# Second layer of a four-layer cross-attention kernel: transposes issued one projection behind the next scores, the output projection in the second and fourth quarter

## The chip, the cores and the metric

The kernel runs on one core of a Trainium2 chip. A core has engines with instruction streams of their own: TensorE (matmuls and transposes, writing to eight PSUM banks), VectorE, ScalarE, GpSimd, and SyncE, which here only issues DMAs. They order each other by semaphores. The metric is the device time of one execution in microseconds (us); lower is better.

## What is computed

Four layers of cross attention run one after the other on x (16 blocks of 128 x 512) with one context (16 x 128 x 512): a latent layer, a grouped-query layer (the one changed here), a cross layer with an MLP, a latent layer again. The second layer is, cut to what matters:

```python
B, L, S = (4, 256, 256)        # 32 heads, 8 key/value heads, 16 wide; per 256 rows
q = hidden_state @ Wq + bq
k = encoder_hidden_state @ Wk + bk
v = encoder_hidden_state @ Wv + bv
...
scores = jnp.einsum('bkgld,bksd->bkgls', q, k) * scale
scores = scores + encoder_attention_mask[:, :, None, :, :]
attn = jax.nn.softmax(scores, axis=-1)
out = jnp.einsum('bkgls,bksd->bkgld', attn, v)
out = out.transpose(0, 3, 1, 2, 4).reshape(b, l, H)
out = out @ Wo + bo
x = out + hidden_state
mu = jnp.mean(x, axis=-1, keepdims=True); var = jnp.var(x, axis=-1, keepdims=True)
return (x - mu) * jax.lax.rsqrt(var + EPS) * gamma + beta
```

(The kernel groups the rows its own way: 16 blocks of 128 rows, taken as 8 pairs, with a mask and context for each.)

## The kernel before

Everything is fp32; weight matmuls run in three passes of a split into a rounded high part and a low rest (`three_passes`, L325, called from everywhere, so L327 carries most matmuls of all kinds). The order of each engine is written out by hand, one function for an engine and a layer: `pe_gqa`, `act_gqa`, `dve_gqa`, `pool_gqa`, `sp_gqa`.

The second layer is a loop over 8 pairs of blocks. A pair has four rounds (k = 0 to 3), each 16 score groups of 128 x 128 on four partition strips: round k treats block k % 2 of the pair and heads half k // 2. One round is:

- scores S(k) on TensorE (`pe_scores`, L418, 24 matmuls of 256 columns) into PSUM banks 0 to 3;
- `dve_max` (L1017) on VectorE for r = 0 to 3: adds the mask, writes the negated scores to SBUF, keeps the maximum, frees the bank;
- `act_exp` (L733) on ScalarE for r = 0 to 3, four exponentials each, with sums;
- `dve_invert` (L1042): reciprocals of the sums, one half (two r) at a time; `pool_norm` (L1370) on GpSimd multiplies them in;
- transposes T(k) (`pe_turn_probs`, L460, 16 of 128 x 128) into four banks; `act_probs` copies banks 0 and 2 to SBUF, `dve_probs` banks 1 and 3;
- attention A(k) (`pe_attend`, L471); its bank is evacuated by `act_heads` (L748, high part) and then `dve_heads` (L1068, low part, which frees the bank and counts as the evacuation).

Banks 4 to 7 are a ring: `begin` (L217) gives every projection, transpose group and attention the next bank, and waits until the one four places back has been evacuated. So TensorE can be no more than four results ahead of the slower of its readers, in the order in which they are issued.

Between the rounds stand the projections: queries Q, keys KG and values VG of the next pair in this layer, keys KC and values VC of the next layer (computed ahead here and stored to DRAM), the turning of the next pair's rows X, and the output projection of a block, O (`pe_out`, L502). `pe_out` waits for the evacuated attention of both rounds of its block: rounds 0 and 2 for the even one, 1 and 3 for the odd one. VectorE adds residual and bias to it (`dve_out`, L1169) and takes its moments; GpSimd normalises twice (`pool_root`, `pool_again`) and adds the next bias (`pool_bias`); SyncE stores and loads (`sp_gqa`, L1677). The context of the next pair is loaded into the place of the present one's (`sp_c`, L1558), once the last projection that reads it has been filled.

TensorE's order in a middle pair before is: S1 T0 X O(odd) A0 KG KC | S2 T1 Q KC A1 | S3 T2 VG VC A2 | S0 of the next pair, T3 O(even) Q A3 VC. Here a bar ends a quarter, and each T stands right behind the next round's scores.

## Time and profile before

| | us |
|---|---|
| median of 3 runs | 2543.95 (2542.75 to 2545.22) |
| the profiled execution | 2550.35 |
| its span, first to last instruction | 2548.4 |
| TensorE busy in the span | 2451.6 (96%) |
| VectorE, ScalarE, GpSimd busy | 1237.0, 1086.8, 1126.2 |
| second layer's loop, first S1 to the last pair's end | 378.8 (809.37 to 1188.17) |

A matmul's end is modelled, so a busy share of TensorE says little of how well it is used; starts are better read against each other. A row of a timeline gives start, length, engine, line, operation, operands, count, and in brackets how long the engine was idle before it and what released it. In a table of stretches the column of the clock is the granted TensorE clock as a share of 2.4 GHz, the mean over the stretch.

### The profile page before, as it was taken

The numbers are of one execution on the slowest core, as the hardware profiler recorded it, in microseconds if no ns is written. First come the engines' busy times: TensorE is split into PE (matmuls) and PEld (weight loads), VectorE is DVE, ScalarE is ACT, GpSimd is POOL, SyncE is SP. The second block draws the span as 40 slices with busy tenths as digits, with TensorE's granted clock in tenths as the row PEclk, the third lists the DMA queues.
The fourth block names the chain that finished last, engine by engine and source line by source line (L and its number), as shares of the span: only waits on it lengthen the run. The fifth ranks groups of instructions, "written<-read, shape, count | busy, mean of one in ns | idle before, by whom it ended". The sixth has DMA issues, their size and how long they took to land.

```text
span 2548.4 us, 48703 instructions
## 1 busy us (share of the span) xinstructions
PE 2451.6 (96%) x18464; PEld 2053.4 (81%) x18464; DVE 1237.0 (49%) x3296; ACT 1086.8 (43%) x3712; POOL 1126.2 (44%) x1972
## 2 busy tenths in 40 slices
PE   7999999999999999998888999999999999999999
PEld 6888887888888878887777788888888888788887
DVE  5565655333224667676666432233555555432332
ACT  4555654111114877877777111111555555311111
POOL 3444445600053887778786630033345433640000
PEclk9999999999999999998899999999999999999999
DMA  4221212311033223323443320122112111330110
GB/s 151 72 67 59 98 37 89 90 50 50 18 100 118 99 84 124 110 92 111 152 161 121 116 91 1 50 88 75 35 63 80 51 51 51 104 100 1 50 33 17
DMA packets 106774, 198.07 MB, mean 78 GB/s; under 512 B 8304, under 2 KB 35632, under 8 KB 103600
## 3 DMA queue, kind: packets, MB, share of 16 engines
q1 hardware_dynamic: 106544, 194.97, 23.0%
q8 instruction: 149, 2.44, 0.4%
q14 instruction: 81, 0.66, 0.1%
HBM read 136.22 MB, written 58.72 MB: 76 GB/s over the span
## 4 chain that ended last, share of the span: by engine, by line
PE 79%; ACT 9%; DVE 4%; POOL 4%; DMA 2%; issue 1%; SPq 0%; DVEq 0%; POOLq 0%
PE banks L327 70%; PE banks L468 5%; ACT plain_high L743 5%; PE banks L498 3%; ACT plain_low L743 2%; POOL plain_high L1378 2%; ACT plain_work L808 1%; DVE stats L1158 1%; PE banks L522 1%; ACT plain_work L727 1%; DMA rounded_work<-ctx_split 1%; POOL rounded_high L318 0%; DMA plain_high<-attention_w 0%; DVE plain_work L1173 0%; DVE plain_high L1028 0%
## 5 line engine op out<-in xcount | busy, mean ns | idle before, releaser
L327 PE MATMUL banks<-rounded_work,rounded_low 128*128 128x512 f32 (+1 forms) x2688 | 533.6, 355 | 9.5 <-DVE rounded_low L1190 9.0
L327 PEld LDWEIGHTS banks<-rounded_work,rounded_low 128*128 128x128 f32 x2688 | 445.7, 199 | 73.6 <-issue 12.4
L836 ACT ACTIVATE plain_work<-banks,columns 128x512 f32<-128x512 f32 x192 | 132.4, 690 | 863.9 <-PE banks L327 856.9
L327 PE MATMUL banks<-rounded_work,rounded_high 128*128 128x512 f32 (+1 forms) x2400 | 482.4, 355 | 2.9 <-DMA rounded_work<-ctx_split 2.9
L327 PEld LDWEIGHTS banks<-rounded_work,rounded_high 128*128 128x128 f32 x2400 | 396.3, 191 | 68.0 <-issue 4.4
L1347 DVE CAST rounded_work<-plain_work 128x512 fp32r<-128x512 f32 x192 | 104.5, 544 | 687.6 <-ACT plain_work L836 672.4
L1378 POOL TENSOR_SCALAR plain_high<-plain_high,inv_sum 128x128 f32<-128x128 f32 (+1 forms) x768 | 298.3, 412 | 304.0 <-DVE inv_sum L1050 303.7
L327 PE MATMUL banks<-rounded_low,rounded_work 128*128 128x512 f32 x1728 | 416.3, 392 | 0.0
L327 PE MATMUL banks<-rounded_high,rounded_work 128*128 128x512 f32 (+1 forms) x1728 | 393.1, 379 | 2.4 <-DVE rounded_work L1349 2.4
L327 PEld LDWEIGHTS banks<-rounded_low,rounded_work 128*128 128x128 f32 x1728 | 321.5, 188 | 70.7 <-issue 4.4
L327 PEld LDWEIGHTS banks<-rounded_high,rounded_work 128*128 128x128 f32 x1728 | 310.1, 189 | 65.7 <-issue 5.7
L1378 POOL TENSOR_SCALAR plain_low<-plain_low,inv_sum 128x128 f32<-128x128 f32 (+1 forms) x512 | 221.2, 455 | 286.4 <-DVE inv_sum L1050 286.3
L1524 POOL TENSOR_TENSOR plain_work<-plain_work 128x512 f32<-128x512 f32 x48 | 68.1, 1449 | 584.0 <-DMA plain_work<-x 392.1
L743 ACT ACTIVATE plain_low<-banks,neg_max 128x128 f32<-128x128 f32 (+1 forms) x512 | 209.4, 459 | 28.0 <-DVE neg_max L1032 28.0
L743 ACT ACTIVATE plain_high<-plain_high,neg_max 128x128 f32<-128x128 f32 x512 | 198.0, 391 | 33.9 <-DVE neg_max L1028 33.9
L1032 DVE TENSOR_REDUCE neg_max<-banks 128x2 f32<-128x512 f32 (+1 forms) x320 | 204.8, 682 | 15.7 <-PE banks L457 15.7
L1349 DVE TENSOR_TENSOR rounded_work<-plain_work,rounded_work 128x512 fp32r<-128x512 f32 x192 | 165.5, 862 | 6.6
L468 PE MATMUL banks<-ident,plain_high 128*128 128x128 f32 x1024 | 139.4, 285 | 25.5 <-POOL plain_high L1378 19.6
L468 PEld LDWEIGHTS banks<-ident,plain_high 128*128 128x128 f32 x1024 | 113.3, 144 | 44.9 <-issue 23.8
L1050 DVE RECIPROCAL inv_sum<-row_sum 128x4 f32<-128x4 f32 (+1 forms) x224 | 41.6, 187 | 221.0 <-ACT plain_high L743 126.2
L327 PEld LDWEIGHTS banks<-rounded_work 32*128 32x128 f32 x3072 | 102.0, 186 | 43.6 <-issue 41.7
L327 PE MATMUL banks<-rounded_work 32*128 32x256 f32 (+1 forms) x3072 | 124.1, 291 | 10.2 <-DVE rounded_work L1104 7.5
(106 smaller groups left out, 3118.7 us busy)
## 6 DMA issues: line engine op xcount, KB each, us to landing
plain_work<-x SPq DMA_DIRECT2D x96, 256.0 KB, 3.0
plain_work<-mlp_w SPq DMA_DIRECT2D x96, 256.0 KB, 2.7
rounded_work<-ctx_split SPq DMA_DIRECT2D x16, 1024.0 KB, 5.9
u<-plain_work SPq DMA_DIRECT2D x48, 256.0 KB, 2.1
plain_work<-u SPq DMA_DIRECT2D x12, 1024.0 KB, 7.0
x<-plain_work SPq DMA_DIRECT2D x48, 256.0 KB, 2.2
plain_work<-attention_w SPq DMA_DIRECT2D x44, 256.0 KB, 2.7
ctx_split<-rounded_work SPq DMA_DIRECT2D x8, 1024.0 KB, 5.6
```

What stands on the lines that cost most here:

```text
L327: mm = pe.matmul(dst, lhs(i), rhs(j), start=first and n == 0, stop=last and n == 2, skip_group_check=True)
L468: mm = pe.transpose(dst[:, t * P:(t + 1) * P], pr[:, r, t * P:(t + 1) * P], ident[:, :])
L498: mm = pe.matmul(dst[32 * r:32 * r + 32, i * P:(i + 1) * P], v, pt[:, r, at:at + P], start=t == 0, stop=t == n_t - 1, skip_group_check=True)
L522: mm = pe.transpose(dst[:, r * P:(r + 1) * P], u_nat[:, r, f * P:(f + 1) * P], ident[:, :])
L743: last = act.activation(pr[:, r, part], pr[:, r, part] if gqa else PS[:, r, part], ACT.Exp, scale=-1.0 if gqa else 1.0, bias=neg_max[:, R ...
L836: act.activation(gelu[:, j % 2, :], bank(key), ACT.Gelu_apprx_tanh, bias=col(m.y, 28 + j)).then_inc(evac_of(key), 1)
L1032: dve.tensor_reduce(neg_max[:, R % 2, r, 0:y.segs], src.rearrange("p (g n) -> p g n", g=y.segs), AX.X, ALU.max, negate=True).then_inc(maxe ...
L1050: dve.reciprocal(inv_sum[:, R % 2, 2 * half:2 * half + 2, 0:y.segs], row_sum[:, R % 2, 2 * half:2 * half + 2, 0:y.segs]).then_inc(inverted, 1)
L1347: dve.tensor_copy(G[:, j % 4, 0, :], gelu[:, j % 2, :]).then_inc(g_hi, 1)
L1349: dve.tensor_tensor(G[:, j % 4, 1, :], gelu[:, j % 2, :], G[:, j % 4, 0, :].bitcast(F32), ALU.subtract).then_inc(g_ready, 1)
L1378: last = pool.tensor_scalar(part, part, inv_sum[:, R % 2, r, g:g + 1], 1.0, ALU.mult, ALU.mult)
L1524: last = pool.tensor_tensor(res[:, r, :], res[:, r, :], wide_bias, ALU.add)
```

## The change

- TensorE: after each S comes first a projection (VC in the first and third quarter, O in the second and fourth), then T. O moves from the first quarter to the second (odd block) and, in the fourth, ahead of T3 (even block); VC moves from the third quarter and the lap's end to the first and third; KC, KG and VG are spread anew. X is waited for by the queries, not by the keys (`pe_rows`).
- ScalarE and VectorE get a round of their own for this layer (`act_late_round`, `dve_late_round`): ScalarE does exponentials 0 and 1, then both copies of turned banks, then exponentials 2 and 3. VectorE does maxima 0 and 1, something handed in (`lower`), maximum 2, something handed in (`beside`), maximum 3, the lower reciprocals, its two copies, something handed in (`behind`), the upper reciprocals. Handed in as `lower` are the heads of round 1 (in round 3), of round 2 (in round 0 of the next pair) and of round 3 (in round 1 of the next pair); the heads of round 0 stay behind the work of round 1.
- The output's addition (`dve_add`) is split from its moments (`dve_added`). Both VC copies are on VectorE.
- GpSimd and SyncE follow: bias, root and repeat change places among the normalisations; the context load stands behind the stores of keys and values and waits for VG instead of VC.

```diff
@@ -348,8 +348,12 @@
                 pe.wait_ge(aff_split, 2 * p + 2)
             else:
                 pe.wait_ge(c_loaded, 16 * (c_index(y, p) + 1))
-                wait_evac(pe, ("X", y.n, p, 0))
-                wait_evac(pe, ("X", y.n, p, 1))
+                if y.kind == LATENT:
+                    pe_rows(pe, y, p)
+
+        def pe_rows(pe, y, p):
+            for i in range(2):
+                wait_evac(pe, ("X", y.n, p, i))
 
         def pe_turn_x(pe, y, p):
...
             if y.kind == CROSS and i == 0:
                 pe_inputs(pe, y, p)
+            if y.kind == GQA and i == 0:
+                pe_rows(pe, y, p)
...
             if p == 0:
                 pe_weights(pe, y, "kv" if y.kind == GQA else "v")
+            if y.kind == CROSS and i == 0:
+                pe.wait_ge(c_loaded, 16 * (c_index(L[1], p) + 1))
@@ -627,41 +635,40 @@
             for p in range(PAIRS):
                 more = p + 1 < PAIRS
                 pe_scores(pe, y, p, 1)
+                if more:
+                    pe_values(pe, L[2], p + 1, 0)
                 pe_turn_probs(pe, y, p, 0)
                 pe_turn_x(pe, *((y, p + 1) if more else (L[2], 0)))
+                if more:
+                    pe_keys(pe, y, p + 1, 0)
+                pe_attend(pe, y, p, 0)
+                if more:
+                    pe_keys(pe, L[2], p + 1, 0)
+                pe_scores(pe, y, p, 2)
                 if p:
                     pe_out(pe, y, 2 * p - 1)
-                pe_attend(pe, y, p, 0)
-                if more:
-                    pe_keys(pe, y, p + 1, 0)
-                    pe_keys(pe, L[2], p + 1, 0)
-                pe_scores(pe, y, p, 2)
                 pe_turn_probs(pe, y, p, 1)
                 pe_queries(pe, *((y, p + 1) if more else (L[2], 0)), 0)
-                if more:
-                    pe_keys(pe, L[2], p + 1, 1)
                 pe_attend(pe, y, p, 1)
                 pe_scores(pe, y, p, 3)
+                if more:
+                    pe_values(pe, L[2], p + 1, 1)
                 pe_turn_probs(pe, y, p, 2)
                 if more:
-                    pe_values(pe, y, p + 1, 0)
-                    pe_values(pe, L[2], p + 1, 0)
+                    pe_keys(pe, L[2], p + 1, 1)
                 else:
                     pe_queries(pe, L[2], 0, 1)
                 pe_attend(pe, y, p, 2)
                 if more:
-                    pe_scores(pe, y, p + 1, 0)
-                else:
-                    pe_scores(pe, L[2], 0, 0)
+                    pe_values(pe, y, p + 1, 0)
+                pe_scores(pe, *((y, p + 1) if more else (L[2], 0)), 0)
+                pe_out(pe, y, 2 * p)
                 pe_turn_probs(pe, y, p, 3)
-                if not more:
+                if more:
+                    pe_queries(pe, y, p + 1, 1)
+                else:
                     pe_turn_x(pe, L[2], 1)
-                pe_out(pe, y, 2 * p)
-                if more:
-                    pe_queries(pe, y, p + 1, 1)
                 pe_attend(pe, y, p, 3)
-                if more:
-                    pe_values(pe, L[2], p + 1, 1)
 
         def pe_cross(pe, y):
@@ -858,6 +865,15 @@
         def act_warm(act, n, func):
 
             act.activation(warm[:, n:n + 1], minus_half[:, :], func)
+
+        def act_late_round(act, y, p, k, turned, of):
+
+            act_exp(act, y, p, k, 0)
+            act_exp(act, y, p, k, 1)
+            act_probs(act, of, *turned, 0)
+            act_probs(act, of, *turned, 2)
+            act_exp(act, y, p, k, 2)
+            act_exp(act, y, p, k, 3)
 
         def act_latent(act, y):
@@ -936,42 +952,35 @@
...
+                act_late_round(act, y, p, 1, (p, 0), y)
+                for i in range(2):
+                    act_x(act, *((y, p + 1) if more else (L[2], 0)), i)
+                if more:
+                    act_keys(act, y, p + 1, 0)
+                act_heads(act, y, p, 0)
+                if more:
+                    act_keys(act, L[2], p + 1, 0)
+                act_late_round(act, y, p, 2, (p, 1), y)
+                act_queries(act, *((y, p + 1) if more else (L[2], 0)), 0)
+                act_heads(act, y, p, 1)
+                act_late_round(act, y, p, 3, (p, 2), y)
+                if more:
+                    act_keys(act, L[2], p + 1, 1)
+                else:
+                    act_queries(act, L[2], 0, 1)
+                act_heads(act, y, p, 2)
+                if more:
+                    act_values(act, y, p + 1, 0)
+                act_late_round(act, *((y, p + 1) if more else (L[2], 0)), 0, (p, 3), y)
+                if more:
+                    act_queries(act, y, p + 1, 1)
+                else:
...
+                        act_x(act, L[2], 1, i)
                 act_heads(act, y, p, 3)
...
@@ -1039,9 +1048,9 @@
         def dve_probs(dve, y, p, k, r):
             dve_copy(dve, ("T", y.round(p, k), r), prob_t(y)[:, r, :])
 
-        def dve_invert(dve, y, p, k):
+        def dve_invert(dve, y, p, k, halves=(0, 1)):
             R, u = y.round(p, k), y.use(p, k)
-            for half in range(2):
+            for half in halves:
                 for r in (2 * half, 2 * half + 1):
                     if y.kind == GQA:
@@ -1166,17 +1175,37 @@
                 dve.tensor_scalar(neg_mean[:, i:i + 1], moments[:, i, 0:1], -1.0, None, ALU.mult)
                 dve.tensor_copy(spread[:, i:i + 1], moments[:, i, 1:2]).then_inc(moments_ready, 1)
 
-        def dve_out(dve, y, b):
+        def dve_add(dve, y, b):
             key = ("out", y.n, b)
             wait_filled(dve, key)
             dve.wait_ge(biased, y.b0 + b + 1)
             dve.tensor_tensor(hidden[:, b % 2, :], bank(key), hidden[:, b % 2, :], ALU.add).then_inc(evac_of(key), 1)
-            wait_evac(dve, key)
+
+        def dve_added(dve, y, b):
+            wait_evac(dve, ("out", y.n, b))
             dve_moments(dve, y, b)
+
+        def dve_out(dve, y, b):
+            dve_add(dve, y, b)
+            dve_added(dve, y, b)
 
         def dve_again(dve, y, b):
             dve.wait_ge(norm_ready, b + 1)
             dve_moments(dve, y, b, 1)
+
+        def dve_late_round(dve, y, p, k, turned, lower, beside, behind, of):
+
+            dve_max(dve, y, p, k, 0)
+            dve_max(dve, y, p, k, 1)
+            lower()
+            dve_max(dve, y, p, k, 2)
+            beside()
+            dve_max(dve, y, p, k, 3)
+            dve_invert(dve, y, p, k, (0,))
+            dve_probs(dve, of, *turned, 1)
+            dve_probs(dve, of, *turned, 3)
+            behind()
+            dve_invert(dve, y, p, k, (1,))
 
         def dve_latent(dve, y):
@@ -1258,45 +1287,59 @@
...
+            for i in range(2):
+                dve_values(dve, L[2], 0, i)
...
+                def values(i):
+                    if more:
+                        dve_values(dve, L[2], p + 1, i)
+
+                def last_heads():
+                    if p:
+                        dve_heads(dve, y, p - 1, 3)
+
+                def cross_keys():
+                    if more:
+                        dve_keys(dve, L[2], p + 1, 0)
+
+                def odd_out():
+                    if p:
+                        dve_add(dve, y, 2 * p - 1)
+
+                def odd_moments():
+                    if p:
+                        dve_again(dve, y, 2 * p - 2)
+                        dve_added(dve, y, 2 * p - 1)
+
+                def even_moments():
+                    if p:
+                        dve_again(dve, y, 2 * p - 1)
+                    dve_added(dve, y, 2 * p)
+
+                dve_late_round(dve, y, p, 1, (p, 0), last_heads, lambda: values(0), nothing, y)
+                for i in range(2):
+                    dve_x(dve, *((y, p + 1) if more else (L[2], 0)), i)
+                if more:
+                    dve_keys(dve, y, p + 1, 0)
                 dve_heads(dve, y, p, 0)
...
+                dve_late_round(dve, y, p, 2, (p, 1), cross_keys, odd_out, odd_moments, y)
                 dve_queries(dve, *((y, p + 1) if more else (L[2], 0)), 0)
+                dve_late_round(dve, y, p, 3, (p, 2), lambda: dve_heads(dve, y, p, 1), lambda: values(1), nothing, y)
...
+                else:
...
+                dve_late_round(dve, *((y, p + 1) if more else (L[2], 0)), 0, (p, 3), lambda: dve_heads(dve, y, p, 2),
+                               lambda: dve_add(dve, y, 2 * p), even_moments, y)
...
+                else:
+                    for i in range(2):
+                        dve_x(dve, L[2], 1, i)
+            dve_heads(dve, y, PAIRS - 1, 3)
...
@@ -1466,12 +1509,7 @@
                 more = p + 1 < PAIRS
                 pool_norm(pool, y, p, 1)
                 if p:
-                    pool_again(pool, y, 2 * p - 2)
-                    pool_root(pool, y, 2 * p - 1)
-                pool_norm(pool, y, p, 2)
-                if p:
-                    pool_again(pool, y, 2 * p - 1)
-                pool_bias(pool, y, 2 * p)
+                    pool_bias(pool, y, 2 * p - 1)
                 if p < 4:
                     split_tile(pool, ("qo", 2), p)
                 if not more:
@@ -1479,12 +1517,19 @@
                     pool.wait_ge(v_stored, 16 * PAIRS)
                     split_tile(pool, ("qo", 2), 4)
                     split_tile(pool, ("qo", 2), 5)
+                pool_norm(pool, y, p, 2)
+                if p:
+                    pool_again(pool, y, 2 * p - 2)
+                    pool_root(pool, y, 2 * p - 1)
                 pool_norm(pool, y, p, 3)
-                pool_bias(pool, y, 2 * p + 1)
+                pool_bias(pool, y, 2 * p)
                 if not more:
                     split_tile(pool, ("qo", 2), 6)
                 pool_norm(pool, *((y, p + 1) if more else (L[2], 0)), 0)
+                if p:
+                    pool_again(pool, y, 2 * p - 1)
                 pool_root(pool, y, 2 * p)
+            pool_bias(pool, y, B - 1)
 
         def pool_cross(pool, y):
@@ -1679,24 +1724,23 @@
             for t, name in ((gamma, "gamma"), (beta, "beta")):
                 sp.dma_start(t, ins[f"L1_xattn_{name}"].rearrange("(a n) -> a n", a=1).broadcast_to([P, D])).then_inc(gb_loaded, 16)
             sp_ahead(sp, 0)
+            wait_filled(sp, ("V", 2, 0, 1))
+            sp_c(sp, y, 1)
             for p in range(PAIRS):
                 more, far = p + 1 < PAIRS, p + 2 < PAIRS
                 if more:
-                    wait_filled(sp, ("V", 2, p, 1))
-                    sp_c(sp, y, p + 1)
                     if p:
                         sp.wait_ge(s_free[3], y.use(p - 1, 3) + 1)
                     sp_qk_mask(sp, p + 1)
                 if p < 4:
                     load_tile(sp, ("qo", 2), p)
                 if not more:
-                    wait_filled(sp, ("V", 2, p, 1))
+                    wait_filled(sp, ("Q", 1, p, 1))
                     sp_cross_keys(sp, 0)
                     sp_mask(sp, L[2], 0)
                     load_tile(sp, ("qo", 2), 4)
                     load_tile(sp, ("qo", 2), 5)
                 if p:
-                    sp_values_ahead(sp, p)
                     sp_store_h(sp, y, 2 * p - 2)
                 if more:
                     wait_filled(sp, ("X", y.n, p + 1, 1))
@@ -1711,10 +1755,14 @@
                     load_tile(sp, ("qo", 2), 6)
                 if p:
                     sp_store_h(sp, y, 2 * p - 1)
+                if more:
+                    sp_ahead(sp, p + 1)
+                if far:
+                    wait_filled(sp, ("V", 1, p + 1, 0))
+                    sp_c(sp, y, p + 2)
+                if p:
                     sp_store_u(sp, y, 2 * p - 1)
                     sp_next_hidden(sp, y, 2 * p + 1)
-                if more:
-                    sp_keys_ahead(sp, p + 1)
 
```

## Rows read from the trace of the kernel before

**Rows 1.** Stretches (laps 0, 6, 7): length; busy PE, PEld, DVE, ACT, POOL; clock; DMA.

```profile
809.37:857.47 48.10, 42.96 (x465) 37.73 (x464) 30.07 (x170) 37.59 (x160) 28.09 (x71) 0.96 0.22 75
...
1095.38:1142.71 47.33, 44.70 (x478) 38.61 (x477) 33.44 (x183) 37.38 (x160) 36.56 (x83) 1.00 0.31 104
1142.71:1188.17 45.46, 36.54 (x405) 30.73 (x404) 29.59 (x144) 34.16 (x155) 37.66 (x78) 0.85 0.30 100
```

**Rows 2.** Timeline of TensorE, lap 5: start, length, operation, count, idle before and releaser.

```profile
1048.05 1.00 PE L327 MATMUL banks<-rounded_work 32*128 32x256 f32 x24
1048.99 1.97 PE L468 MATMUL banks<-ident,plain_high 128*128 128x128 f32 x16
1050.79 1.36 PE L359 MATMUL banks<-ident,plain_work 128*128 128x128 f32 x8
1052.43 3.00 PE L327 MATMUL banks<-rounded_high 128*128 128x512 f32 x12 [0.29 <-ACT plain_work L727]
1055.37 1.08 PE L498 MATMUL banks<-plain_work 128*32 128x128 f32 x32
1056.38 1.69 PE L327 MATMUL banks<-rounded_work,rounded_high 128*128 128x256 f32 x12
1057.91 3.04 PE L327 MATMUL banks<-rounded_work,rounded_low 128*128 128x256 f32 x24
1060.88 1.00 PE L327 MATMUL banks<-rounded_work 32*128 32x256 f32 x24
...
1071.46 0.66 PE L468 MATMUL banks<-ident,plain_high 128*128 128x128 f32 x4
...
1074.67 2.87 PE L327 MATMUL banks<-rounded_high,rounded_work 128*128 128x128 f32 x24
...
1082.20 1.09 PE L468 MATMUL banks<-ident,plain_high 128*128 128x128 f32 x8
...
1085.58 3.01 PE L327 MATMUL banks<-rounded_high 128*128 128x512 f32 x12
...
1095.38 1.00 PE L327 MATMUL banks<-rounded_work 32*128 32x256 f32 x24
```

**Rows 3.** Page, costliest groups: busy us and mean ns of one, idle before.

```profile
L1378 POOL TENSOR_SCALAR plain_high<-plain_high,inv_sum 128x128 f32<-128x128 f32 (+1 forms) x768 | 298.3, 412 | 304.0 <-DVE inv_sum L1050 303.7
L743 ACT ACTIVATE plain_high<-plain_high,neg_max 128x128 f32<-128x128 f32 x512 | 198.0, 391 | 33.9 <-DVE neg_max L1028 33.9
```

**Rows 4.** Timeline of ScalarE, the same lap.

```profile
1065.56 0.58 ACT L727 ACTIVATE plain_work<-banks 128x512 f32<-128x512 f32 x1
```

**Rows 5.** Timeline of VectorE, the same lap.

```profile
1049.06 0.29 DVE L1028 CUSTOM_DVE_ANT_0 plain_high<-banks,plain_work 128x128 f32<-128x128 f32 x1
...
1049.91 0.29 DVE L1028 CUSTOM_DVE_ANT_0 plain_high<-banks,plain_work 128x128 f32<-128x128 f32 x1
...
1054.35 1.29 DVE L1127 TENSOR_TENSOR rounded_work<-banks,rounded_work 128x512 fp32r<-128x512 f32 x2 [0.62 <-ACT rounded_work L812]
...
1073.61 0.60 DVE L1077 SCALAR_TENSOR_TENSOR rounded_high<-banks,columns,rounded_high 128x128 fp32r<-128x128 f32 x2
```

**Rows 6.** Timeline of TensorE, behind three lone gaps elsewhere.

```profile
789.99 1.49 PE L327 MATMUL banks<-rounded_work 32*128 32x256 f32 x24 [1.89 <-issue]
...
1438.76 4.58 PE L327 MATMUL banks<-rounded_high,rounded_work 128*128 128x512 f32 x12 [2.37 <-DVE rounded_work L1349]
...
1780.92 1.01 PE L327 MATMUL banks<-rounded_work 32*128 32x256 f32 x24 [2.04 <-DVE rounded_work L1104]
```

**Rows 7.** Stretches behind the same gaps.

```profile
790.00:795.40 5.40, 5.40 (x49) 5.17 (x50) 3.47 (x32) 3.03 (x16) 0.00 (x0) 0.68 0.00 0
...
1438.70:1442.00 3.30, 3.24 (x8) 2.59 (x9) 3.23 (x4) 0.69 (x1) 3.13 (x4) 0.52 0.14 22
...
1780.90:1784.00 3.10, 3.08 (x37) 2.64 (x38) 1.98 (x4) 1.25 (x5) 0.00 (x0) 1.00 0.00 0
```

**Rows 8.** Chain of waits, in lap 0: start, length, what.

```profile
810.69 7.42 DMA rounded_work<-ctx_split
```

54 lines of the change are left out of this document (6 added, 48 removed).

## Prediction

> **What bounds the kernel now.** I read the page's busy shares first: TensorE is by far the busiest. The change touches only the second layer, so I went there with the table of stretches, cut at the first scores of each pair (a lap: from S1 of one pair to S1 of the next). Laps 1 to 6 run from 857.47 to 1142.71, 47.54 us each; lap 0 takes 48.10, lap 7 45.46 with a granted clock of 0.85 [rows 1]. In a middle lap TensorE is busy 44.70 of 47.33, with the clock at 1.00, GpSimd 36.56, ScalarE 37.38, VectorE 33.44: no other engine fills a lap.
>
> Then TensorE's own timeline shows what the lap could lose [rows 2]. Sixteen transposes at their own pace take 1.80 us (1048.99 to 1050.79). In the third quarter they take 3.21 (1071.46 to 1074.67), in the fourth 3.38 (1082.20 to 1085.58), and the eight of the input rows 1.64 where half of 1.80 would do. That is 1.41 + 1.58 + 0.74 = 3.73 us of waiting and refilling a lap; without it the lap would be 43.6. Six laps of 3.7 are 22 us, the most that this change could bring.
>
> **The change part by part.** I name TensorE's steps S (scores), T (transposes), A (attention), Q, KG and VG (this layer), KC and VC (next layer's keys and values), X (rows), O (output). The new lap is S1 VC T0 X KG A0 KC | S2 O(odd) T1 Q A1 | S3 VC T2 KC A2 VG | S0 O(even) T3 Q A3. TensorE's work is the same; only its order and what it waits for differ.
>
> *Removed: the waits of T.* The transposes of a quarter now start S + one 12-step projection after the next scores, 0.94 + 2.94 = 3.9 us [rows 2]. In a quarter the sixteen exponentials take 16 x 0.39 = 6.2 us of ScalarE [rows 3]; now the two lower ones come first and the copies after them, all done 9.15 after the scores (worked out below), and GpSimd's last eight multiplications take 8 x 0.41 = 3.3 at most (a mean that mixes two sizes): 12.8 with 0.3 for the inverse. The last T is due 13.5 + 1.3 after its scores (quarter 9.6 + 3.9). So I take all 3.73 as gone. In the first and third quarter, 12 us long, GpSimd's root and repeat stand ahead of the multiplications, and T is due 16 us after its scores there. The bias is due when O is done; GpSimd has 10 us a lap to spare [rows 1], so I cost it at nothing; late by x, it costs x.
>
> *Added: X waits for copies, KC for X.* The ring has four banks, so KC needs the bank of the first X. VectorE frees it only after ScalarE has done exponentials 0 and 1, two copies (0.5 each [rows 4]) and exponentials 2 and 3. In time from S1: maxima from 1.0, 0.85 each; exponentials from 1.95, the first two done at 5.05, copies at 6.05, all done at 9.15; VectorE's subtraction starts 0.62 after ScalarE's copy of X and takes 0.69 for the first [rows 5], free at 10.5. KC would be due at 0.94 + 2.94 + 1.80 + 0.9 + 0.3 + 1.53 + 1.01 = 9.4 (the 0.3 is the second X waiting for VectorE's copy). So a wait of 1.0 besides the 0.3.
>
> *Added: O(even) waits for the heads, and this decides.* `pe_out` waits for the evacuated attention of both quarters of its row, the newer being A2. VectorE's half of that evacuation (`dve_heads`) is now handed to the next round as `lower`: behind the maxima of scores 0 and 1 of S0. TensorE however issues O right behind S0. Those maxima start 1.0 us after S0 and take 1.70, the heads 0.60 [rows 5]: free at 3.3, O starts at about 3.45 where S0 ended at 0.94. A wait of 2.5 us in each lap. Queued behind it on TensorE are T3, Q, A3 and the next S1; on VectorE the addition of O, and behind that maximum 3 and the inverses. What is late next is only O itself; nothing else runs on TensorE meanwhile. Before, the heads of A2 were done well ahead, since O came after T3. O(odd) has no such wait: its last heads are done in the first quarter.
>
> Two more bank waits (Q behind T, KC behind T2) are 0.1 each. New waits: 0.3 + 1.0 + 0.2 + 2.5 = 4.0, and 0.2 for refilling the array: lap 43.6 + 4.2 = 47.8, against 47.54, so +0.26. Freed waits and new ones cancel.
>
> *The clock.* A gap of 2.5 us is new for a middle lap. Three lone gaps in dense work show what follows one [rows 6, 7]: after 1.89 us idle the granted clock is 0.68 over the next 5.4 us, after 2.37 it is 0.52, near 1.2 GHz, after 2.04 it stays at 1.00, 2.4 GHz. The twelve 512-wide matmuls after the second took 4.58 against 2.94 [rows 2, 6]: 1.6 us lost, on the path, as O stands behind the gap. Two of three gaps: 1.1 per lap. Bounds 0 and 1.6. The Trainium skill (TensorE: Matmul & The Clock Gate, section "Why this matters for your kernels") warns of long idle stretches of TensorE, not of pauses as short as these; by it the clock would hold here, and two of three rows disagree. With it: +0.26 - 0 instead of +1.36 per lap. The laps go by the rows: 6 x 1.36 = 8.2.
>
> *Lap 0.* The next pair's VC now comes straight behind S1, and needs that pair's context, whose place is free only when this pair's VC has been computed. The load was issued at 810.69 and took 7.42, to 818.1 [rows 8]; before, T0, X and A0 ran meanwhile. Now TensorE stands still from 810.3 to 818.1, then VC runs at the low clock (4.45 with its overlap, to 822.55). VectorE holds maximum 3 until it has copied VC. T fills a bank in 0.6; ScalarE copies it at 823.2 and the third at 824.05, does exponentials 2 and 3 by 827.65, X is freed 1.3 later, KC runs to 832.0. The other three quarters have 43.6 - 12.1 = 31.5 of work and 2.9 of waits: S1 of lap 1 at 866.4, not 857.47, +8.9; with the clock behind O, +10.0. A context landing sooner and VC at full clock would make it 6.5 or so.
>
> *Later context loads* are issued when VG is done, at S0, and needed 13 us later; they took 7.4 with other transfers beside them [rows 8]. The keys' and values' stores now start about 1.5 us before it. I cost it at nothing; late by x, it costs x a lap.
>
> *Lap 7 and the next layer's head.* T1 no longer waits behind row work, and O(14) waits 2.4 for its heads. I take 0, between -3 and +3.
>
> *Moved at no cost:* one value copy from ScalarE to VectorE (0.6 us of 14 idle [rows 1]); root, repeat and bias on GpSimd; on SP the context load now stands behind the stores of keys and values and a store of the result.
>
> **The sum.** 10.0 + 8.2 + 0 = +18.2 us on the profiled execution, whose own time is 2550.35 (2548.4 and 1.95 around it), 6.4 over the median of 2543.95. The difference carries over: 2562.1.
>
> **The rivals.**
> - *The clock holds:* seven laps lose 1.1 less, 18.2 - 7.7 = 10.5, giving 2554.5. For it: the gap of 2.04 and the 1.00 of every middle lap; against: two of three gaps. 0.25. This is what the rule of the Trainium skill above would give.
> - *Faster: the heads are free in time.* If VectorE reached A2's heads before S0, O would not wait: lap 45.3, six laps -13.4, lap 0 +6.4, sum -7.0: 2536.9. It decides at a wait w of 7w = 7.0, 1.0 us. Against it stands the order: maxima 0 and 1 alone are 1.7 long. 0.07.
> - *No change:* laps stay at 47.5 with the clock up, and lap 0 loses 5 or less: 2546 or so. 0.11.
> - *The context load becomes the bound.* Taking twice its 7.42 beside the stores, it is late by 1.8 in each of six laps: 18.2 + 10.8, 2573. For it: 1.5 MB more at the same time; against: 13 us of room. 0.05.
>
> **How the numbers follow.** Forecast 2562.1, chance 0.52. A measurement of this kernel can't tell less than 0.2% (5.1 us) from no change. Slower: 0.52 + 0.25 + 0.05 = 0.82; same 0.11; faster 0.07. Low end: no fall of the clock, lap 0 at 7, lap 7 at -3: +5.0, 2549. High end: the clock falls in all seven laps (+3.5) and lap 7 gives +3: 2569.
>
> **What would show it.** Right: eight waits of TensorE of about 2.5 us at the output on VectorE's heads; about 1 us a lap on VectorE's subtraction of X; no wait of T on GpSimd in laps 1 to 6; laps of 48 to 49.5 with a clock between 0.93 and 1.00; lap 0 near 57 to 58 with one wait of 7 to 8 us on the context. Wrong: laps near 45 (the heads don't hold O), or waits of VC on the context in every lap.

## The result, and the profile after

The changed kernel takes 2572.97 us (median of 4 runs, 2569.33 to 2573.43); the kernel before took 2544.59 beside it. The ratio is 1.0112 with a 95% interval of 1.0097 to 1.0126: slower by 28.4 us, where +18.2 was forecast. The sign and the main mechanism came out as predicted, the size did not: 2572.97 lies above the range, which ended at 2569.

The profiled execution took 2572.71 with a span of 2570.5. TensorE's busy share is still 96%, so it shows nothing. The laps do, each cut from the S1 of one pair to the S1 of the next as in [rows 1]. Columns: stretch, length, busy time of PE (TensorE), PEld (its weight loads), DVE (VectorE), ACT (ScalarE) and POOL (GpSimd), granted clock, DMA share, GB/s moved. The stretches are laps 0, 1, 2, 6, 7 and the first pair of the third layer.

```profile
805.35:864.73 59.38, 46.43 (x465) 40.77 (x464) 30.04 (x168) 36.75 (x157) 23.86 (x61) 0.89 0.29 94
864.73:912.68 47.95, 44.45 (x480) 39.13 (x477) 34.12 (x184) 37.20 (x160) 37.51 (x83) 1.00 0.26 90
912.68:962.22 49.54, 46.06 (x480) 40.24 (x477) 33.99 (x184) 37.18 (x160) 38.88 (x86) 0.97 0.32 105
...
1110.52:1160.08 49.56, 46.08 (x480) 40.33 (x477) 34.04 (x184) 37.18 (x160) 36.34 (x83) 0.97 0.22 79
1160.08:1207.41 47.33, 36.69 (x408) 30.93 (x405) 30.67 (x149) 34.56 (x153) 42.00 (x87) 0.86 0.24 85
1207.41:1239.50 32.09, 25.78 (x284) 21.67 (x280) 17.55 (x44) 20.06 (x93) 27.15 (x50) 0.89 0.41 149
```

Lap 0 has grown by 11.3. A middle lap is 47.95 where the clock stays at 1.00 and 49.4 to 49.6 where it falls; of laps 1 to 6 only the first keeps it. The last lap and the third layer's first pair together take 79.42.

TensorE's timeline of lap 5 (and one row of lap 1) shows what a middle lap waits for now; the rows answer to [rows 2]. A bracket gives the idle time before a row and what released it.

```profile
904.14 2.97 PE L327 MATMUL banks<-rounded_high 128*128 128x512 f32 x12 [2.40 <-issue]
...
1071.61 3.13 PE L327 MATMUL banks<-rounded_work,rounded_low 128*128 128x256 f32 x24 [1.03 <-DVE rounded_work L1136]
...
1078.45 1.94 PE L476 MATMUL banks<-ident,plain_high 128*128 128x128 f32 x16
...
1097.12 1.00 PE L327 MATMUL banks<-rounded_work 32*128 32x256 f32 x24
1100.53 4.43 PE L327 MATMUL banks<-rounded_high 128*128 128x512 f32 x12 [2.41 <-issue]
1104.80 1.91 PE L476 MATMUL banks<-ident,plain_high 128*128 128x128 f32 x16
```

In a middle lap all sixteen transposes of each quarter run without a pause: that part of the change does what it says. In their place stand a wait of 1.03 at the next layer's keys (KC), for VectorE's subtraction of the rows, and one of 2.41 at the even output. Its twelve matmuls take 4.43 there and 2.97 in lap 1 behind an equal pause. That is the clock, as the stretches around the output of lap 1 (2.97) and lap 2 (4.29) show:

```profile
904.10:907.00 2.90, 2.85 (x13) 2.36 (x14) 0.78 (x8) 1.80 (x10) 0.00 (x0) 1.00 1.02 323
952.00:956.20 4.20, 4.13 (x13) 3.15 (x14) 0.81 (x8) 1.82 (x10) 0.00 (x0) 0.67 0.80 267
```

The row of the 2.41 names no releaser ("issue"); VectorE's timeline of the same moment does. These are its first row of the first maximum, and the heads of round 2:

```profile
1098.13 0.29 DVE L1037 CUSTOM_DVE_ANT_0 plain_high<-banks,plain_work 128x128 f32<-128x128 f32 x1 [2.78 <-PE banks L327]
...
1099.82 0.60 DVE L1086 SCALAR_TENSOR_TENSOR rounded_high<-banks,columns,rounded_high 128x128 fp32r<-128x128 f32 x2
```

VectorE stands idle for 2.78 us, takes two maxima, then does the heads until 1100.42; the output starts at 1100.53.

### The profile page after: what moved, and what is told of

Read it like the earlier page. It is cut to its first block, busy times and chain, and to the rows that moved or that the text cites. A ratio compares the mean times of both kernels' runs of the same rounds, so it can differ in the third digit from the quotient of the medians.

```text
span 2570.5 us, 48710 instructions
## 1 busy us (share of the span) xinstructions
PE 2458.4 (96%) x18464; PEld 2064.0 (80%) x18464; DVE 1257.1 (49%) x3304; ACT 1085.1 (42%) x3704; POOL 1124.3 (44%) x1972
## 4 chain that ended last, share of the span: by engine, by line
PE 84%; ACT 7%; DVE 3%; POOL 2%; DMA 2%; issue 1%; SPq 0%; DVEq 0%; POOLq 0%
PE banks L327 73%; PE banks L476 6%; ACT plain_high L750 3%; PE banks L506 3%; ACT plain_low L750 2%; POOL plain_low L1421 1%; ACT plain_work L815 1%; PE banks L530 1%; ACT plain_work L734 1%; POOL rounded_high L318 0%; DMA plain_high<-attention_w 0%; ACT plain_low L734 0%; PE banks L465 0%; DVE plain_high L1037 0%; DVE rounded_work L1113 0%
## 5 line engine op out<-in xcount | busy, mean ns | idle before, releaser
L476 PE MATMUL banks<-ident,plain_high 128*128 128x128 f32 x1024 | 128.7, 279 | 8.7 <-POOL plain_high L1421 3.7
L327 PEld LDWEIGHTS banks<-rounded_work 32*128 32x128 f32 x3072 | 102.3, 186 | 40.4 <-issue 37.5
L1037 DVE CUSTOM_DVE_ANT_0 plain_high<-banks,plain_work 128x128 f32<-128x128 f32 x512 | 114.6, 285 | 31.8 <-PE banks L327 31.8
```

Source lines behind the costliest of these rows:

```text
L327: mm = pe.matmul(dst, lhs(i), rhs(j), start=first and n == 0, stop=last and n == 2, skip_group_check=True)
L476: mm = pe.transpose(dst[:, t * P:(t + 1) * P], pr[:, r, t * P:(t + 1) * P], ident[:, :])
L1037: last = dve.tensor_tensor_reduce(pr[:, r, part], src[:, part], qk_mask[:, p % 2, b, :], -1.0, 3.0e38, ALU.add, ALU.min, accum_out=neg_max ...
```

## The experiments

The table gives the stretches of every profile, each from TensorE's timeline, cut as above; the last column is the median time with its ratio to the kernel before in the same set of runs (medians of before: 2544.59, 2541.66, 2543.20, 2543.06) and the 95% interval of that ratio. A stretch is of one execution, a median of several.

| kernel | lap 0 | laps 1 to 6 | lap 7 + first pair of layer 3 | time, ratio [95%] |
|---|---|---|---|---|
| before | 48.10 | 285.24 | 73.63 | |
| before, again | 47.54 | 285.43 | 71.19 | 2542.46 (one run) |
| after | 59.38 | 295.35 | 79.42 | 2572.97, 1.0112 [1.0097, 1.0126] |
| after, again | 59.30 | 295.36 | 79.63 | 2571.50, 1.0114 [1.0098, 1.0129] |
| heads first | 53.92 | 274.51 | 75.22 | 2543.48, 1.0008 [0.9998, 1.0018] |
| heads mid | 56.02 | 286.97 | 77.18 | 2561.00, 1.0076 [1.0057, 1.0095] |
| rows early | 57.89 | 293.49 | 77.72 | 2569.32, 1.0110 [1.0093, 1.0127] |
| lap 0 old | 55.56 | 295.13 | 80.09 | 2566.06, 1.0094 [1.0079, 1.0109] |
| lap 0 new | 52.36 | 296.80 | 80.20 | 2566.72, 1.0096 [1.0077, 1.0116] |
| values first | 59.30 | 295.35 | 76.36 | 2567.70, 1.0104 [1.0089, 1.0119] |
| values 0 | 56.96 | 293.83 | 79.74 | 2568.96, 1.0105 [1.0086, 1.0123] |
| repeat early | 57.00 | 295.32 | 74.21 | 2570.49, 1.0105 [1.0091, 1.0120] |
| four moves | 49.72 | 269.20 | 72.67 | 2527.78, 0.9941 [0.9926, 0.9956] |
| four moves b | 47.21 | 268.94 | 71.94 | 2523.78, 0.9928 [0.9915, 0.9940] |

### The two kernels once more

Nothing is edited here; the question is how much one profile can be trusted.

> The kernel before, unchanged, profiled once more. Theory (the 6.4 us by which its first profiled execution stood over the median lay in that execution, most of it ahead of the second layer, where the kernels do not differ): the first scores of lap 0 start at 805 to 806.5, not 809.37; laps 1 to 6 are 47.3 to 47.75 again. Rival (the excess lay in the laps): laps of 47.0 or less, and a start of lap 0 at 809.

> The changed kernel, unchanged, profiled once more beside the others on one chip. Theory (waits are fixed by the order, falls of the clock are not): the waits at the even output are 2.40 again in each lap and the wait for the values 4.2; laps differ from 49.4 only by the clock, 48.0 where it holds. Time 1.010 to 1.012 of the kernel before.

Before, again:

```profile
805.20:852.74 47.54, 43.19 (x465) 37.99 (x464) 30.14 (x170) 37.65 (x160) 28.55 (x71) 0.96 0.22 76
...
1138.17:1183.55 45.38, 36.77 (x406) 30.83 (x405) 29.89 (x145) 35.04 (x157) 37.61 (x78) 0.85 0.30 100
1183.55:1209.36 25.81, 22.70 (x285) 19.04 (x281) 18.24 (x44) 18.63 (x86) 23.63 (x44) 1.00 0.46 164
```

Lap 0 starts at 805.20, not 809.37, the middle laps agree within 0.2 us in all six together, and the third layer's first pair takes 25.81 where the first profile had 28.17. So of the 8.0 us between the two spans 4.2 lay ahead of lap 0, 0.6 in lap 0, 2.4 at the layer's end and 1.0 behind it. The second profile of the changed kernel repeats the first within 0.1 in each of laps 0 to 6. Against the second profile of before, the change costs 11.8 in lap 0, 9.9 in laps 1 to 6, 8.2 at the end and 0.1 elsewhere, 30.1 in all; the medians differ by 28.4.

That repetition is not the rule, however. Two of the kernels below, values 0 and repeat early, have the same code as the changed kernel in lap 0, and take 56.96 and 57.00 there, not 59.3: the clock holds in the second and the fourth quarter, where it falls in both profiles of the changed kernel. In laps 1 to 6, too, the falls lie in other laps from kernel to kernel, and the same code took 293.83 (values 0) to 296.80 (lap 0 new). So of the differences between two rows of the table, up to 2.4 us in lap 0 and 3.0 us in laps 1 to 6 can be the clock's.

### The heads ahead of the maxima, and half way

```diff
+                dve_heads(dve, y, p, 2)
                 dve_late_round(dve, *((y, p + 1) if more else (L[2], 0)), 0, (p, 3),
-                               lambda: dve_heads(dve, y, p, 2),
+                               nothing,
                                lambda: dve_add(dve, y, 2 * p), even_moments, y)
```

> The changed kernel with one move: VectorE does its half of the heads of round 2 ahead of the first maximum of the next scores, not behind the second. Theory (the heads' place in VectorE's order holds the output): VectorE is idle for 2.8 us there and ScalarE's half is done before the scores begin, so the waits of 2.40 to 2.56 us at the even output vanish in laps 0 to 6, and so does the fall of the clock behind them (1.2 to 1.5 us in six of the seven laps). Laps of 49.5 become 45.5 to 46; with lap 0 and some of lap 7 the time falls by 24 to 28, to about 2546. Rival (the output would be held by something else, such as the reader of a ring bank or the bias): the wait stays over 1 us and the time falls by less than 10.

The second kernel leaves the heads in the round, behind maximum 0 and not behind maximum 1.

> The changed kernel with VectorE's heads of round 2 one maximum earlier: behind the first maximum of the next scores, not the second. The wait at the even output falls from 2.40 by one maximum (0.85) to about 1.55. Theory (the wait is that order and nothing else): the six middle laps and laps 0 and 7 each lose 0.85, 7 in all, to 2566, if the clock still falls behind a pause of 1.55; if such a pause leaves the clock at 1.00, another 1.4 in each of six laps, to 2558. Rival (something else releases the output): the wait stays at 2.4 and the time at 2573.

TensorE's waits in the middle laps, summed (line waiting, released by, us, times, longest): first the kernel before, then the changed one, then the heads first.

```profile
PE banks L468 <- POOL plain_high L1378: 8.4, 12, 0.8
PE banks L468 <- DVE rounded_work L1104: 5.0, 6, 0.8
PE banks L327 <- ACT plain_work L727: 1.7, 6, 0.3
```

```profile
PE banks L327 <- issue: 14.4, 6, 2.4
PE banks L327 <- DVE rounded_work L1136: 6.1, 6, 1.0
```

```profile
PE banks L327 <- DVE rounded_work L1136: 6.1, 6, 1.1
```

With the heads first the six waits are gone, nothing takes their place, laps are 45.73 to 45.78 with the clock at 1.00, and the time falls by 27, to that of before, as the theory had it. The rival falls. Half way the wait is 1.56, 0.85 less, to the hundredth what one maximum takes; the time, 2561.0, lies between the two that were expected, because the clock neither always falls nor always holds. It falls in laps 1, 3 and 5 and holds in 2, 4 and 6, behind equal pauses. TensorE's output in laps 1 and 2, and the clock of the stretches around them:

```profile
901.51 4.48 PE L327 MATMUL banks<-rounded_high 128*128 128x512 f32 x12 [1.56 <-issue]
...
950.11 3.02 PE L327 MATMUL banks<-rounded_high 128*128 128x512 f32 x12 [1.56 <-issue]
```

```profile
901.40:905.00 3.60, 3.49 (x9) 2.79 (x10) 1.69 (x17) 2.71 (x15) 0.64 (x1) 0.55 1.01 317
950.00:953.60 3.60, 3.49 (x18) 2.95 (x19) 2.13 (x18) 2.71 (x15) 0.65 (x1) 1.00 1.00 302
```

### The rows earlier

```diff
+                def rows():
+                    for i in range(2):
+                        act_x(act, *((y, p + 1) if more else (L[2], 0)), i)
+
-                act_late_round(act, y, p, 1, (p, 0), y)
-                for i in range(2):
-                    act_x(act, *((y, p + 1) if more else (L[2], 0)), i)
+                act_late_round(act, y, p, 1, (p, 0), y, rows)
...
-                dve_late_round(dve, y, p, 1, (p, 0), last_heads, lambda: values(0), nothing, y)
-                for i in range(2):
-                    dve_x(dve, *((y, p + 1) if more else (L[2], 0)), i)
+                dve_late_round(dve, y, p, 1, (p, 0), last_heads, lambda: values(0), rows, y)
```

On ScalarE the call stands between the copies and exponential 2.

> The changed kernel with the copies of the turned rows taken earlier: on ScalarE between the copies of turned banks and exponentials 2 and 3, on VectorE ahead of the upper reciprocals. Theory (the next layer's keys wait for the first row bank): the wait of 1.02 us at the keys goes, laps of 49.4 become 48.4, the time falls by 6 to 8, to about 2566. Rival (the later exponentials pass the microsecond on): the transposes of the second quarter then wait for GpSimd by about 1 us, and the time stays within 2 of 2573.

The wait at the keys is gone and the first quarter is 1.07 shorter (13.53 to 12.46 from S1 to S2); no transpose waits for GpSimd. Yet laps 1 to 6 lose only 1.9 in all, not 6.4, and the ratio of 1.0110 can't be told from the changed kernel's 1.0112 and 1.0114, where 6 to 8 us were expected. Neither side was right: behind the unchanged pause at the output the clock here falls in all six laps, and in laps 3 and 6 it costs 2.8 each. Laps 1 and 6:

```profile
862.94:911.41 48.47, 46.00 (x480) 40.27 (x477) 33.91 (x184) 37.41 (x160) 37.40 (x83) 0.96 0.26 89
...
1106.72:1156.43 49.71, 47.23 (x481) 41.04 (x477) 34.07 (x184) 37.41 (x160) 36.31 (x83) 0.93 0.22 78
```

Whether the longer falls come of taking away the pause of 1.02, or lie in this one execution, stays open.

### Lap 0

```diff
-                if more:
+                if p and more:
                     pe_values(pe, L[2], p + 1, 0)
                 pe_turn_probs(pe, y, p, 0)
                 pe_turn_x(pe, *((y, p + 1) if more else (L[2], 0)))
-                if more:
+                if p and more:
                     pe_keys(pe, y, p + 1, 0)
                 pe_attend(pe, y, p, 0)
+                if not p:
+                    pe_values(pe, L[2], p + 1, 0)
+                    pe_keys(pe, y, p + 1, 0)
```

ScalarE's and VectorE's copies follow.

> The changed kernel with the order of the first quarter of the first lap alone put back: transposes, rows and attention first, then the next pair's values and keys. Theory (in lap 0 TensorE stands still for the context): the wait of 6.72 us goes, lap 0 falls from 59.4 to 48 to 50, the time by 9 to 11, to about 2563; later laps are as they were, 49.4. Rival (lap 0 is long because of its second quarter, where no output stands between scores and transposes): lap 0 stays above 54.

Lap 0 falls by 3.8 only, to 55.56, on the rival's side, and the time by about 5, not 9 to 11. The context's wait is gone and the first quarter takes 16.65, not 21.85; but the clock falls for longer in the fourth (14.97, not 13.59), and TensorE's rows show what came in the wait's place:

```profile
812.00 1.87 PE L363 MATMUL banks<-ident,plain_work 128*128 128x128 f32 x8 [2.85 <-ACT plain_work L737]
...
826.54 0.66 PE L476 MATMUL banks<-ident,plain_high 128*128 128x128 f32 x4 [1.17 <-DVE rounded_low L1109]
828.69 4.59 PE L327 MATMUL banks<-rounded_work,rounded_high 128*128 128x256 f32 x24 [1.50 <-ACT plain_work L737]
```

The rows' transposes need the bank of the first T, and ScalarE now copies it only behind exponentials 0 and 1: in the new round a T straight behind its scores costs 2.85 at the next ring bank. The second quarter has the same shape in either kernel, as pair 0 has no odd output to stand between S2 and T1: 1.17, 1.50, and here queries at the low clock. With the clock up it is no longer than a middle lap's, as the waits stand where the output would: in the nine profiles that have this quarter it takes 11.33 where the clock falls (four) and 9.84 where it holds (five). The rival's reason is thus worth 1.5 us, and not in every execution. So the next kernel gives lap 0 a projection in both places that needs no new context: the upper queries of pair 0 (before, ahead of the loop) behind S1, the next layer's first keys behind S2.

```diff
-            pe_queries(pe, y, 0, 1)
...
                 pe_scores(pe, y, p, 1)
-                if more:
+                if not p:
+                    pe_queries(pe, y, 0, 1)
+                elif more:
                     pe_values(pe, L[2], p + 1, 0)
...
                 pe_attend(pe, y, p, 0)
-                if more:
+                if not p:
+                    pe_values(pe, L[2], p + 1, 0)
+                    pe_keys(pe, y, p + 1, 0)
+                elif more:
                     pe_keys(pe, L[2], p + 1, 0)
                 pe_scores(pe, y, p, 2)
                 if p:
                     pe_out(pe, y, 2 * p - 1)
+                else:
+                    pe_keys(pe, L[2], p + 1, 0)
...
-            sp_ahead(sp, 0)
+            sp_keys_ahead(sp, 0)
             wait_filled(sp, ("V", 2, 0, 1))
             sp_c(sp, y, 1)
+            sp_values_ahead(sp, 0)
```

> The changed kernel with the first lap filled with work that needs no context of the next pair: the upper queries of pair 0 stand between its second scores and the transposes (not ahead of the loop), values and keys of the next pair behind the attention, the next layer's first keys behind the third scores; the context's load is issued ahead of the store of values. Theory (a transpose needs a projection ahead of it in lap 0 as in every other lap, and the context needs 7 to 8 us of other work): the waits of 6.72 us on the context and of 2.7 us in the second quarter go, lap 0 falls from 59.4 to 47 to 50, and the stretch ahead of it by up to 3: 2558 to 2562. Rival (lap 0 would be long in any order, by the reader of the ring banks): lap 0 stays above 54, as with the old order.

Lap 0 is 52.36, with 3 us of queries more in it than in the changed kernel: 7.0 less than in that kernel's profiles, 4.6 less than in those where the clock held; the expectation was 47 to 50. A wait of 2.34 is left in the second quarter, where VectorE's split of this layer's keys holds back the maxima. With keys and values exchanged there lap 0 goes from 49.72 to 47.21 between the two combinations below. The time, 2566.72, misses the expected 2558 to 2562; in this profile all six middle laps fall to the low clock, and the end takes 80.2.

### The end of the layer

The chain of waits of the changed kernel names what its last stretch hangs on (start, length, what):

```profile
1208.69 4.22 POOL plain_low L1421 x8
...
1213.93 0.78 POOL plain_work L1462
1214.72 0.32 SPq L1621
1215.14 0.38 SPq L1610
1215.56 0.46 SPq L1717
1216.06 0.43 SPq L306
1216.54 6.96 DMA plain_work<-cross_values
...
1223.63 1.93 PE banks L506 x32
```

GpSimd multiplies the next layer's first round, then does the repeat of block 13 (L1462); SyncE's store of that block waits for it, and behind the store stand the loads of keys and values of the third layer, then rows and mask. Its first attention waits 4.20 for the values. Before, the repeat stood ahead of those multiplications and the values' load was issued 5.0 after S1 of the third layer, here 9.1. Three edits test this. The first issues store and next load behind the values' loads:

```diff
-                if p:
+                if p and more:
                     sp_store_u(sp, y, 2 * p - 1)
                     sp_next_hidden(sp, y, 2 * p + 1)
...
             sp_cross_values(sp, 0)
             sp_cross_values(sp, 1)
+            sp_store_u(sp, prev, B - 3)
+            sp_next_hidden(sp, prev, B - 1)
```

> The changed kernel with one move on SyncE: at the end of the second layer the store that waits for GpSimd's repeat of block 13, and the load behind it, are issued after the loads of the next layer's values, not before. Theory (the queue stood behind the repeat, and so the values came late): the values' load is issued some 8 us sooner, TensorE's wait of 4.20 us for it goes, and the stretch from the last S1 to the second pair of the next layer falls from 79.4 to 73 to 75; time 2567 to 2569. Rival (the load is held by the place it writes to, free only after the last attention): the wait stays above 3 us and the time does not move by 2.

The wait falls to 1.31 and the stretch by 3.1, where 4.4 to 6.4 were expected: the load is issued only 3 us sooner, since the keys ahead of it wait for the next rows to be split (`aff_split`). And in the pair behind, T waits for GpSimd, which stood at the bias of block 15 for its late rows:

```profile
1242.66 1.09 PE L476 MATMUL banks<-ident,plain_low 128*128 128x128 f32 x4 [4.53 <-POOL plain_low L1421]
```

The second leaves the store and moves only the first values' load ahead of it:

```diff
+                if not more:
+                    wait_filled(sp, ("O", y.round(p, 3)))
+                    sp_cross_values(sp, 0)
                 if p:
                     sp_store_u(sp, y, 2 * p - 1)
```

> The changed kernel with only the load of the next layer's first values moved on SyncE: ahead of the store that waits for GpSimd's repeat of block 13; that store and the load behind it keep their place ahead of everything else. Theory (the store of block 13 holds the queue, and the store's move in the earlier experiment made the bias of block 15 late): the load is issued when the last attention is done, some 8 us sooner than in the changed kernel, the wait of 4.20 us goes and no wait of 4.5 us on GpSimd takes its place; 5 to 7 us less, 2566 to 2568. Rival (another wait of the next layer stands behind it): the wait goes and the time does not fall by more than 2.

The wait for the values is gone and nothing is won: 79.74, where the four profiles without an edit of the last lap gave 79.42 to 80.20. That is the rival. The chain now runs through another load behind the same store, that of the mask, whose handling on VectorE (L1161) stands ahead of the queries' evacuation, for which TensorE's next scores wait (last row, of its timeline):

```profile
1215.56 5.74 DMA plain_work<-mask_BxS_bf
1221.33 0.05 DVE plain_work L1161
...
1223.47 2.85 PE L327 MATMUL banks<-rounded_work 32*128 32x128 f32 x48 [2.87 <-DVE rounded_work L1113]
```

The third takes away the reason: GpSimd's repeat of block 13 comes ahead of the multiplications of the next layer, and VectorE's second moments of it move to the end of round 3.

```diff
                 pool_norm(pool, y, p, 3)
+                if not more:
+                    pool_again(pool, y, 2 * p - 1)
                 pool_bias(pool, y, 2 * p)
...
-                if p:
+                if p and more:
                     pool_again(pool, y, 2 * p - 1)
```

> The changed kernel with one move in the last lap: VectorE takes the second moments of block 13 at the end of round 3, and GpSimd does that block's repeat behind the multiplications of round 3, not behind those of the next layer's first round. Theory (that repeat holds a store on SyncE, and behind the store the loads of keys, values, rows and mask of the next layer): all of these are issued some 10 us sooner, the wait of 4.20 us for the values goes and no wait for the mask takes its place; lap 7 and the next layer's first pair take 73 to 76, not 79.4, and the time falls by 3 to 6. Rival (the next layer's start is bound by its own order): the stretch stays above 78.

The stretch takes 74.21, 5.2 less, as expected. SyncE's queue shows why it isn't more: the store leaves at 1198.45, ahead of S1 of the third layer at 1205.76, but the keys still wait for the split rows. So the values go out 5.8 after that S1, not 9.1 (3.4 sooner, where some 10 were expected; 5.0 in the kernel before), and TensorE keeps a wait of 1.12.

```profile
1198.45 0.32 SPq L1627 DMA_DIRECT2D x_unit<-plain_work  x1
...
1210.69 0.32 SPq L1723 DMA_DIRECT2D rounded_work<-cross_keys  x1
...
1211.53 1.17 SPq L1726 DMA_DIRECT2D plain_work<-cross_values  x2
```

The time does not show it: the median of 2570.49 against 2571.50 of the changed kernel in the same set is less than these few runs can tell apart, not the 3 to 6 that were expected. The profiled execution took 2564.09, the other three 2570.26 to 2572.25, so the gain is shown for that one execution; that the queue is the cause rests on its stretch.

### All four together

> All moves together: heads of round 2 ahead of the first maximum, rows copied early, the first values' load ahead of the store, lap 0 filled. Theory (the change's own gain of 3.7 us a lap is there, and these four places had eaten it): middle laps of 44.7 at a clock near 1.00, lap 0 of 45 to 47, no wait for the values; 2514 to 2522, faster than the kernel before by 0.9 to 1.1 per cent. Rival (each removed wait shows up at the next reader or in the clock): laps of 46 or more and a time of 2535 or more.

> The four moves together, with the repeat of block 13 early in place of the values' load ahead of the store, and in lap 0 the keys ahead of the values behind the first attention. Theory: middle laps of 44.7 to 44.9 as before, lap 0 of 48 to 49.5, lap 7 and the next layer's first pair 68 to 72; 2 to 5 us less than the first combination, 2522 to 2526. Rival (the last stretch is bound by GpSimd's multiplications, which now come later): no gain on the first combination, 2527 to 2530.

Four moves b has the heads first, the rows early, the repeat early and lap 0 filled. A middle lap and lap 0:

```profile
806.93:854.14 47.21, 44.96 (x490) 39.70 (x489) 30.93 (x170) 37.02 (x159) 23.86 (x61) 1.00 0.36 119
...
898.85:943.69 44.84, 44.77 (x480) 39.16 (x477) 34.03 (x184) 37.20 (x160) 38.85 (x86) 1.00 0.35 116
```

TensorE is busy 44.77 of 44.84 and no wait is left in laps 1 to 6. The time is 2523.78, 0.9928 of before (0.9915 to 0.9940): 19 us faster, and 48 faster than the changed kernel in the same set. The stretches account for that: against the changed kernel's second profile they give 12.1 in lap 0, 26.4 in laps 1 to 6 and 7.7 at the end, 46.2 together. The first combination was expected at 2514 to 2522 and gave 2527.78: its laps are as expected, lap 0 (49.72, expected 45 to 47) is not, and at its end a wait of 3.02 for the mask is left, as in the kernel with the values' load alone. The second lies within its 2522 to 2526, with lap 0 shorter than its 48 to 49.5 and the end at the edge of its 68 to 72.

## Why the prediction was right, and where it was wrong

Against the first profile of before, on which the sum was made, and against the second:

| term | forecast | against the first | against the second |
|---|---|---|---|
| lap 0 | +10.0 | +11.3 | +11.8 |
| laps 1 to 6 | +8.2 | +10.1 | +9.9 |
| lap 7 and the next layer's head | 0 | +5.8 | +8.2 |
| ahead of lap 0, and behind the third layer's first pair | 0 | -5.1 | +0.1 |
| sum | +18.2 | +22.1 | +30.1 |

- **The waits of T go:** right, but sized too large. None is left, in any of laps 1 to 6. The 3.73 us a lap were taken from the distances between starts, against T's best pace. The waits that the trace names (the first of the three lists of waits above) come to 15.1 in six laps, 2.5 a lap, and 2.7 a lap came back: with the four moves the lap without waits is 44.8 (47.5 before), not 44.0 (43.6 with 0.4 of small waits and refilling). T, rows and several projections take 0.05 to 0.2 more from start to start than at the pace of [rows 2], for a reason that no run here isolates; no run shows the 0.2 for refilling by itself either.
- **O(even) waits for the heads:** right, in place, cause and size: 2.40 for 2.5. Moving one call of `dve_heads` takes it away, and moving it by one maximum takes that maximum off. The rival in which the heads are free in time gave laps of 45.3 and 2536.9; made so, the kernel has laps of 45.75 and takes 2543.48, as lap 0 and the end stay long.
- **KC waits for the rows:** right, 1.02 for 1.0; the further 0.3 did not come.
- **A middle lap** of 47.95 at full clock, forecast 47.8: near, and partly by luck. The work is 0.8 longer than forecast (44.8, not 44.0), the new waits add 3.1, not 3.8.
- **The clock:** right in kind, too small. It was weighted with two of three [rows 6, 7]; behind the pauses of 2.40 it fell in 5 of 6 laps, 1.5 us each, and in 41 of 48 over the eight profiles that have them. Behind 1.56 it fell in 3 of 6, behind 1.02 alone in none of 6. The rival in which it holds, 2554.5, is out.
- **Lap 0:** the wait for the context came (6.72; 7.8 forecast), and the first quarter took 21.85, where the sum has 22.6. The other three were set at 34.4 (31.5 of work and 2.9 of waits) and 1.1 for the clock, and took 37.5. The difference is the clock: it fell in the fourth quarter and, where no fall was reckoned with, in the second. In values 0 and repeat early it holds in both, the three quarters take 34.5 and lap 0 takes 57.0. So the +11.3 is one of two outcomes of the same code, and the forecast of +10.0 lies between them. The 34.4 itself was met by luck: it counts 2.9 of work for an odd output, which pair 0 does not have, and leaves out the waits of 1.17 and 1.50 that stand in its place. The rows of the changed kernel, and the last two rows again from values 0:

```profile
813.07 4.78 PE L327 MATMUL banks<-rounded_low,rounded_work 128*128 128x512 f32 x12 [6.72 <-DMA rounded_work<-ctx_split]
...
824.13 3.14 PE L327 MATMUL banks<-rounded_work,rounded_low 128*128 128x256 f32 x24 [0.82 <-DVE rounded_work L1136]
...
830.83 0.66 PE L476 MATMUL banks<-ident,plain_high 128*128 128x128 f32 x4 [1.17 <-DVE rounded_low L1104]
832.99 4.61 PE L327 MATMUL banks<-rounded_work,rounded_high 128*128 128x256 f32 x24 [1.50 <-ACT plain_work L734]
...
854.71 4.46 PE L327 MATMUL banks<-rounded_high 128*128 128x512 f32 x12 [2.56 <-DVE rounded_high L1086]
```

```profile
832.59 3.11 PE L327 MATMUL banks<-rounded_work,rounded_high 128*128 128x256 f32 x24 [1.50 <-ACT plain_work L734]
...
852.80 2.98 PE L327 MATMUL banks<-rounded_high 128*128 128x512 f32 x12 [2.55 <-DVE rounded_high L1086]
```

- **Lap 7 and the next layer's head:** the step that failed. It was taken as 0, between -3 and +3, from TensorE's waits alone, and "root, repeat and bias on GpSimd" were moved at no cost. It cost 5.8, or 8.2 against the second profile, the largest miss of the sum. Lap 7 has 1.9 of that (47.33 against 45.46): the wait at its even output is not made up, and with the heads first lap 7 takes 45.46 again. (In three other profiles the split is another, 49.4 for lap 7 and 30.3 to 30.8 for the pair behind it, with the same total of about 80.) The rest, 3.9 or 6.3, lies in the third layer's first pair: 32.09, against 28.17 and 25.81. In the middle laps no run shows a cost of the moved repeat. In the last one the repeat holds a store on SyncE, and the store holds every load that the third layer starts with; with the repeat early that pair takes 26.72. The sum did not ask who queues behind a GpSimd step that is moved back past sixteen multiplications.
- **Later context loads:** right, no VC waits for the context in laps 1 to 6. The rival built on them gave 2573, the time that came, but its mechanism is nowhere in the trace.
- **The carry-over:** the difference was to be made against one profile's own time, 6.4 over the median. That is sound only if the excess lies outside the stretches compared; 2.4 of it lay in the last stretch and 0.6 in lap 0, so that the first profile shows those losses too small.
- **The range:** its low end adds up to +5.6 (1.6, 7 and -3), not +5.0; that changes nothing here. Its high end left 3 us for the last stretch, which took 5.8 to 8.2.

## What to carry to other kernels

Putting a projection between scores and transposes removes a wait only if that projection has its own inputs ready; ask of every step put early which engine finishes its newest input, and where in that engine's order this stands. A loop's first and last pass need a sum of their own: a wait that every middle pass hides came out where an operand, or a neighbour in the order, is missing. When a step is moved back on one engine, follow the queues that wait for it, stores included, to the last load behind them.

## What the runs showed of the hardware

- Behind equal pauses in equal work the granted clock may hold or fall: with 1.56 us idle it alternated from lap to lap (0.55 and 1.00 over the 3.6 us around the output), with 2.40 it fell in 41 of 48 laps. A fall costs 1.4 to 1.6 us here, at times 2.8. The Trainium skill (TensorE: Matmul & The Clock Gate, section "Why this matters for your kernels") warns of long idle stretches; here pauses of 1.56 us were enough at times, and the measurement decides.
- In the one profile without the pause of 1.02 us, the falls behind the other pause came in all six laps and cost 2.8 in two of them (a clock of 0.93 over the lap, against 0.96 to 0.97), so that 1.9 us of 6.4 was kept. That the missing pause is the reason is not shown.
- Two executions of one kernel agreed within 0.1 us in each of laps 1 to 6, while 4.2 us of difference sat ahead of them in code that is the same. Other executions of the same lap 0 took 59.38, 59.30, 56.96 and 57.00: a small difference between two profiles is read against the clock first.
